# Attention: q and k from one projection of 128 stationary columns, and weight subtraction in four pieces

## What is computed

```python
def _L0_conv_ref(x, Wq, bq, Wk, bk, Wv, bv, alpha):      # B, C, H, W = 4, 256, 32, 32; MID = C // 8 = 32
    xf = x.reshape(b, c, n)
    q = jnp.einsum('mc,bcn->bmn', Wq, xf) + bq[None, :, None]
    k = jnp.einsum('mc,bcn->bmn', Wk, xf) + bk[None, :, None]
    v = jnp.einsum('oc,bcn->bon', Wv, xf) + bv[None, :, None]
    energy = jnp.einsum('bmi,bmj->bij', q, k)
    wmat = jax.nn.softmax(energy, axis=-1)
    y = jnp.einsum('bcj,bij->bci', v, wmat)
    return alpha[0] * y + x
...
t = t + _L1_attn_ref(_ln_t(t), L1_attn_proxy)
t = t + _L1_ffn_ref(_ln_t(t), gate_w, w1, b1, w2, b2)    # 8 experts, 2 for each token
```

## Time and profile before

| | us |
|---|---|
| median of 3 runs | 785.04 (781.91 to 786.17) |
| profiled execution, its own time | 785.2 |
| its span, first to last instruction | 783.5 |
| first instruction of stage B (SyncE's load, line 796) | at 221.23 |
| busy: PE, DVE, ACT, POOL | 714.9, 441.9, 331.9, 407.3 |

### The profile page before, as it was taken

How to read it: one execution, slowest core, us unless ns; L and a number is a source line. 1 busy time by engine, 2 the same in 40 slices (tenths; PEclk the granted TensorE clock), 3 DMA queues, 4 the chain that set the end, 5 groups by cost and what they waited for, 6 DMA issues and landing times.

```text
span 783.5 us, 18460 instructions
## 1 busy us (share of the span) xinstructions
PE 714.9 (91%) x5438; PEld 679.2 (87%) x5439; DVE 441.9 (56%) x1049; ACT 331.9 (42%) x640; POOL 407.3 (52%) x480
## 2 busy tenths in 40 slices
PE   5899999999939887489999999999999999999993
PEld 4899898998917665379999999999999999999993
DVE  3675666757636999625454554455454454454541
ACT  2674755747516677333323323323233233233230
POOL 1474565787662443263456556555565465555233
PEclk9999999999969999679999999999999999999997
DMA  7759578496460333222656535665476275373122
GB/s 244 244 175 399 216 264 341 165 352 248 162 256 28 111 109 110 83 77 76 209 157 195 183 82 177 182 197 155 149 236 173 48 227 177 53 225 79 20 29 30
DMA packets 45872, 130.14 MB, mean 166 GB/s; under 512 B 5184, under 2 KB 35520, under 8 KB 41216
## 3 DMA queue, kind: packets, MB, share of 16 engines
q1 hardware_dynamic: 30560, 104.86, 36.1%
q0 software_dynamic: 13904, 19.45, 14.3%
q10 hardware_dynamic: 1360, 5.24, 1.7%
HBM read 186.80 MB, written 47.59 MB: 299 GB/s over the span
## 4 chain that ended last, share of the span: by engine, by line
PE 54%; issue 1%; DMA 1%; POOL 1%; DVE 0%; POOLq 0%; ACT 0%; DVEq 0%
PE ps_h L73 9%; PE ps_h L74 9%; PE ps_h L75 9%; PE ps_y L73 8%; PE ps_y L74 8%; PE ps_y L75 8%; PE ps_x L1599 2%; DMA out_tok<-y,to_row 0%; POOL out_tok L1474 0%; DMA x_rows<-normed,from_row 0%; POOLq L1397 0%; DVE yb L1554 0%; DVE xtl L1534 0%; DVE y L1561 0%; ACT xth L1499 0%
## 5 line engine op out<-in xcount | busy, mean ns | idle before, releaser
L1508 ACT ACTIVATE g<-ps_h,bias 128x256 f32<-128x256 f32 x288 | 120.7, 471 | 279.5 <-PE ps_h L75 279.4
L1474 POOL DMA_INDIRECT out_tok<-y,to_row x72 | 126.9, 1762 | 140.2 <-DVE y L1561 119.7
L73 PE MATMUL ps_h<-xth,wbuf 128*128 128x256 f32 x576 | 164.6, 286 | 3.3 <-issue 1.8
L73 PE MATMUL ps_y<-wbuf,gl 128*128 x576 | 164.5, 286 | 0.0
L74 PE MATMUL ps_h<-xtl,wbuf 128*128 128x256 f32 x576 | 164.4, 285 | 0.0
L75 PE MATMUL ps_h<-xth,wbuf 128*128 128x256 f32 x576 | 163.1, 283 | 0.0
L75 PE MATMUL ps_y<-wbuf,gh 128*128 x576 | 161.6, 281 | 0.0
L74 PE MATMUL ps_y<-wbuf,gh 128*128 x576 | 161.6, 281 | 0.0
L73 PEld LDWEIGHTS ps_h<-xth,wbuf 128*128 128x128 f32 x576 | 109.6, 190 | 3.7 <-issue 2.1
L75 PEld LDWEIGHTS ps_h<-xth,wbuf 128*128 128x128 f32 x576 | 110.9, 193 | 0.0
L74 PEld LDWEIGHTS ps_h<-xtl,wbuf 128*128 128x128 f32 x576 | 109.8, 191 | 0.0
(11 more groups left out here) (241 smaller groups left out, 1297.0 us busy)
## 6 DMA issues: line engine op xcount, KB each, us to landing
wbuf<-wsplit SPq DMA_DIRECT2D x71, 2048.0 KB, 8.1
wsplit<-wbuf SPq DMA_DIRECT2D x14, 2048.0 KB, 12.0
wraw<-in_w SPq DMA_DIRECT2D x16, 1024.0 KB, 7.6
raw<-in_x_ch ACTq DMA_DIRECT2D x5, 1024.0 KB, 9.0
normed<-x SPq DMA_DIRECT2D x8, 528.0 KB, 3.0
tok<-in_x_tok SPq DMA_DIRECT2D x1, 4096.0 KB, 16.7
out_tok<-tok SPq DMA_DIRECT2D x8, 512.0 KB, 3.8
x_rows<-normed,from_row POOLq DMA_INDIRECT x72, 3.4
```

What stands on the lines that cost most here:

```text
L73: eng.matmul(out, ll, rh, start=first, stop=False)
L1474: pool.indirect_dma_start(out=out, out_offset=bass.IndirectOffsetOnAxis(ap=to_row[:, par, s:s + 1], axis=0), in_=y[:, par, s, :], in_offse ...
L1508: last = act.activation(g[:, f, :], ps_h[:, q, f % 2, :], ACT.Gelu_apprx_tanh, bias=bias1[:, bass.ds(e, 1), f:f + 1].rearrange("p a f -> p ...
```

## The change

One matrix of 128 stationary columns, Wq twice and Wk twice, replaces the two of 96. One projection of 12 matmuls gives all of q and k in `ps_sc`: rows 0 to 63 hold q twice, rows 64 to 127 hold k twice. It stands before the weighted sum of tile 6; the second projection, before tile 7, is gone, and `ps_pt[0]` isn't used for it. ScalarE makes the high parts with two activations of 64 partitions, both before the last weight part of the image. VectorE makes the low part of q in rows 32 to 63 and copies its high part to rows 64 to 95; it makes the low part of k in rows 64 to 95 and copies the high part, which stands in rows 96 to 127, to rows 0 to 31 and 32 to 63. That is three copies of 32x1024 for each image that were not there. Apart from that, GpSimd's subtraction of the weights is cut into four instructions of 128x512, the last of which signals.

```diff
@@ stage_a
-        wqh, wql = sb("wqh", [P, 2, KT, 3 * MID], F32R), sb("wql", [P, 2, KT, 3 * MID], F32R)
+        wqh, wql = sb("wqh", [P, KT, P], F32R), sb("wql", [P, KT, P], F32R)
-        qk3 = sb("qk3", [3 * MID, 2, N], F32R)
+        qk3 = sb("qk3", [P, 2, N], F32R)
@@ sync
-            for kind in range(2):
-                sp.dma_start(wq_raw[:, kind], wqk3[kind].rearrange("(k p) m -> p k m", p=P)).then_inc(wqk_in, 16)
+            sp.dma_start(wq_raw, wqk4.rearrange("(k p) m -> p k m", p=P)).then_inc(wqk_in, 16)
@@ gpsimd
-                        pool.tensor_tensor(wbuf[:, par, at + n:at + 2 * n], wraw[:, part],
-                                           wbuf[:, par, at:at + n].bitcast(F32), ALU.subtract).then_inc(w_lo, 1)
+                        m = n // PIECES
+                        for i in range(PIECES):
+                            last = pool.tensor_tensor(wbuf[:, par, at + n + i * m:at + n + (i + 1) * m],
+                                                      wraw[:, part, i * m:(i + 1) * m],
+                                                      wbuf[:, par, at + i * m:at + (i + 1) * m].bitcast(F32), ALU.subtract)
+                        last.then_inc(w_lo, 1)
@@ scalar
-            def high_qk(b, kind):
-                act.wait_ge(qk_mm, done(b * 2 + kind))
+            def high_qk(b):
+
+                act.wait_ge(qk_mm, done(b))
                 act.wait_ge(scored, done(b * IT - 1))
-                act.activation(qk3[:, kind], (ps_sc, ps_pt[0])[kind][0:3 * MID, :], ACT.Identity,
-                               bias=bqk[:, kind:kind + 1]).then_inc(qk_hi, 1)
+                for kind in range(2):
+                    at = slice(kind * 2 * MID, (kind + 1) * 2 * MID)
+                    act.activation(qk3[at, kind], ps_sc[at, :], ACT.Identity, bias=bqk[at, 0:1]).then_inc(qk_hi, 1)
@@
                     if it == 7 and more:
-                        high_qk(b + 1, 0)
+                        high_qk(b + 1)
@@
-                if more:
-                    high_qk(b + 1, 1)
@@ vector
-                at = slice(MID, 2 * MID) if kind == 0 else slice(2 * MID, 3 * MID)
+                low = slice((kind + 1) * MID, (kind + 2) * MID)
+                src, copies = ((0, (2,)), (3, (0, 1)))[kind]
                 dve.wait_ge(qk_hi, done(b * 2 + kind))
-                dve.scalar_tensor_tensor(out=qk3[at, kind], in0=(ps_sc, ps_pt[0])[kind][at, :], scalar=bqk[at, kind:kind + 1],
-                                         in1=qk3[at, kind].bitcast(F32), op0=ALU.add, op1=ALU.subtract).then_inc(qk_ok, 1)
+                dve.scalar_tensor_tensor(out=qk3[low, kind], in0=ps_sc[low, :], scalar=bqk[low, 0:1],
+                                         in1=qk3[low, kind].bitcast(F32), op0=ALU.add, op1=ALU.subtract)
+                for row in copies:
+                    last = dve.tensor_copy(qk3[row * MID:(row + 1) * MID, kind], qk3[src * MID:(src + 1) * MID, kind])
+                last.then_inc(qk_ok, 1)
@@ tensor
                 for n in range(N // HALF):
                     cols = slice(n * HALF, (n + 1) * HALF)
                     for k in range(KT):
-                        last = mm3(pe, dst[0:3 * MID, cols], (wqh[:, kind, k], wql[:, kind, k]),
-                                   (xh[:, k, cols], xl[:, k, cols]), k == 0, k == KT - 1)
+                        last = mm3(pe, ps_sc[:, cols], (wqh[:, k], wql[:, k]), (xh[:, k, cols], xl[:, k, cols]),
+                                   k == 0, k == KT - 1)
@@
-                        last = pe.matmul(ps_sc[:, cols], qk3[:, 0, it * P:(it + 1) * P], qk3[:, 1, cols],
+                        last = pe.matmul(ps_sc[:, cols], qk3[0:3 * MID, 0, it * P:(it + 1) * P], qk3[0:3 * MID, 1, cols],
@@
-                    if more and it >= IT - 2:
-                        project_qk(b + 1, it - (IT - 2))
+                    if more and it == IT - 2:
+                        project_qk(b + 1)
                     weigh(it)
@@ kernel
-        "wqk3": np.stack([np.tile(wq.T, (1, 3)), np.tile(wk.T, (1, 3))]),
+        "wqk4": np.concatenate([wq.T, wq.T, wk.T, wk.T], axis=1),
```

More of the change, by code:

```diff
@@ L42 @@
 EARLY = 2
+PIECES = 4
 FT = F // P
@@ L182, in chunk_tiles, with build @@
     return chunk_of(tok.t[:, :, :], c)[:, :, 0:C]
-def build(nc, x_ch, x_tok, wqk3, bqk3, wv_t, wv, bv, bv_t, alpha, proxy_t, gate_t, w1, b1_t, w2, b2, out):
+def build(nc, x_ch, x_tok, wqk4, bqk4, wv_t, wv, bv, bv_t, alpha, proxy_t, gate_t, w1, b1_t, w2, b2, out):
     wsplit = nc.dram_tensor("wsplit", [E, P, WROW], F32, kind="Internal").ap()
@@ L202, in build @@
         stage_a(nc, sem, tok, wbuf, ident, fixed, xraw, wsplit, normed, proxy_t, gate_t,
-                x_ch, x_tok, wqk3, bqk3, wv_t, wv, bv, bv_t, alpha, w1, w2)
+                x_ch, x_tok, wqk4, bqk4, wv_t, wv, bv, bv_t, alpha, w1, w2)
         tabs = keep("tabs", [P, 7, PAIRS], I32)
@@ L211, in stage_a @@
 def stage_a(nc, sem, tok, wbuf, ident, fixed, xraw, wsplit, normed, proxy_t, gate_t,
-            x_ch, x_tok, wqk3, bqk3, wv_t, wv, bv, bv_t, alpha, w1, w2):
+            x_ch, x_tok, wqk4, bqk4, wv_t, wv, bv, bv_t, alpha, w1, w2):
     with ExitStack() as ctx:
@@ L218, in stage_a @@
         xh, xl = sb("xh", [P, KT, N], F32R), sb("xl", [P, KT, N], F32R)
-        wqh, wql = sb("wqh", [P, 2, KT, 3 * MID], F32R), sb("wql", [P, 2, KT, 3 * MID], F32R)
-        bqk = sb("bqk", [3 * MID, 2])
+        wqh, wql = sb("wqh", [P, KT, P], F32R), sb("wql", [P, KT, P], F32R)
+        bqk = sb("bqk", [P, 1])
         wvh, wvl = sb("wvh", [P, KT, VW], F32R), sb("wvl", [P, KT, VW], F32R)
@@ L239, in early @@
             return wraw[:, 1, at:at + n].rearrange(spec, **sizes)
[L241 to L244, removed]
+        wq_raw = early(0, [KT, P], "p (k m) -> p k m", k=KT)
+        wv_raw = early(KT * P, [KT, VW], "p (k m) -> p k m", k=KT)
+        wv_nat = early(KT * P + KT * VW, [KT, C], "p (k m) -> p k m", k=KT)
+        zero_row = early(KT * P + KT * VW + KT * C, [PAD // P, XW], "p (k m) -> p k m", k=PAD // P)
         ps_sc = ctx.enter_context(nc.psum_tensor("ps_sc", [P, N], F32))
@@ L279, in _ @@
             sp.dma_start(bv_col, bv_t).then_inc(ext_in, 16)
-            for kind in range(2):
-                sp.dma_start(wq_raw[:, kind], wqk3[kind].rearrange("(k p) m -> p k m", p=P)).then_inc(wqk_in, 16)
-            sp.dma_start(bqk[:, :], bqk3).then_inc(consts, 16)
+            sp.dma_start(wq_raw, wqk4.rearrange("(k p) m -> p k m", p=P)).then_inc(wqk_in, 16)
+            sp.dma_start(bqk[:, :], bqk4).then_inc(consts, 16)
             sp.dma_start(wv_raw[:, :, 0:C], wv_t.rearrange("(k p) m -> p k m", p=P)).then_inc(consts, 16)
@@ L470, in _ @@
             act.wait_ge(consts, 64)
-            high_qk(0, 0)
-            high_qk(0, 1)
+            high_qk(0)
             images(act, image)
@@ L484, in _ @@
             last.then_inc(bv_spread, 1)
-            dve.wait_ge(wqk_in, 32)
-            dve.tensor_copy(wqh[:, :, :, :], wq_raw).then_inc(wsm_hi, 1)
+            dve.wait_ge(wqk_in, 16)
+            dve.tensor_copy(wqh[:, :, :], wq_raw).then_inc(wsm_hi, 1)
             dve.wait_ge(wsm_hi, 1)
-            dve.tensor_tensor(wql[:, :, :, :], wq_raw, wqh[:, :, :, :].bitcast(F32), ALU.subtract).then_inc(wsm_ok, 1)
+            dve.tensor_tensor(wql[:, :, :], wq_raw, wqh[:, :, :].bitcast(F32), ALU.subtract).then_inc(wsm_ok, 1)
             for k in range(KT):
@@ L613, in _, with project_qk @@
             pe.wait_ge(ident_ok, 1)
[L615 to L622, removed]
+            def project_qk(b):
+                pe.wait_ge(x_split, b + 2)
+                pe.wait_ge(exped, done(b * IT - 1))
                 for n in range(N // HALF):
@@ L686, in image @@
                         turn(it + 1)
-                    if more and it >= IT - 2:
-                        project_qk(b + 1, it - (IT - 2))
+                    if more and it == IT - 2:
+                        project_qk(b + 1)
                     weigh(it)
-            project_qk(0, 0)
-            project_qk(0, 1)
+            project_qk(0)
             pe.wait_ge(wsm_ok, 2)
@@ L1647, in _ @@
             all_pairs(pe, run)
-INPUTS = ["x_ch", "x_tok", "wqk3", "bqk3", "wv_t", "wv", "bv", "bv_t", "alpha", "proxy_t", "gate_t", "w1", "b1_t", "w2", "b2"]
+INPUTS = ["x_ch", "x_tok", "wqk4", "bqk4", "wv_t", "wv", "bv", "bv_t", "alpha", "proxy_t", "gate_t", "w1", "b1_t", "w2", "b2"]
 def kernel(x, L0_conv_Wq, L0_conv_bq, L0_conv_Wk, L0_conv_bk, L0_conv_Wv, L0_conv_bv, L0_conv_alpha,
@@ L1663 @@
         "x_tok": flat.transpose(0, 2, 1).reshape(TOK, C),
-        "wqk3": np.stack([np.tile(wq.T, (1, 3)), np.tile(wk.T, (1, 3))]),
-        "bqk3": np.stack([np.tile(np.asarray(L0_conv_bq), 3), np.tile(np.asarray(L0_conv_bk), 3)], axis=1),
+        "wqk4": np.concatenate([wq.T, wq.T, wk.T, wk.T], axis=1),
+        "bqk4": np.concatenate([np.asarray(b) for b in (L0_conv_bq, L0_conv_bq, L0_conv_bk, L0_conv_bk)])[:, None],
         "wv_t": wv.T,
```

## The result

The changed kernel takes 791.13 us (median of 5 runs, 789.77 to 792.23), the kernel before 785.27 us (5 runs, 781.91 to 786.17) beside it: ratio 1.0093, 95% interval 1.0069 to 1.0118. It is slower by 5.9 us. The prediction was 788.5, in a range of 783 to 794. It called a result above 789.0 slower and gave that 0.40, against 0.51 for the same: 791.13 is on the slower side. The profiled execution took 790.25 us, with a span of 788.5.

What follows compares the result with a forecast made beforehand. TensorE, busy 43.56 of 45 us, was taken to bound the attention stage. Start -0.3, passages between images +0.95, +0.95, +0.5 and end +1.4 sum to +3.5 on 785.04: 788.5 us, range 783 to 794.

Steps and rivals of the forecast that it cites:

- the clock: TensorE's new waits: granted clock drops to 0.50, one drop costing about 2 us, 790.5 to 792; chance 0.10.
- The projection: TensorE, each image: one of two 12-matmul projections goes, 128 columns cost nothing extra; 2.8 us saved, 11 us in all.
- The order at a passage: From one image to the next: engine times from t0, the image's last transposes; TensorE ends v's first part at +12.2, then waits.
- Do the copies wait for GpSimd?: Between images: VectorE copies wait for GpSimd's running piece, at most 1.29 us each; taken as +0.95, +0.95, +0.5.
- Rival 1: Between images: copies run beside GpSimd without collision; -1.6 us in all, 783.6; chance 0.20.
- rival 3: Between images: GpSimd isn't interrupted, copies wait through all four pieces; about +11.5 us, 796.5; chance 0.12.
- Rival 2: Between images: q and k ready before TensorE asks, near -2.1 us each; -5.2 in all, 780; chance 0.08.
- The second maximum 5.1 us after q and k are ready: Next image's start: VectorE's second row maximum comes 5.1 us after q and k are ready, against t0 +19.05 before.
- The start: Start of the attention stage: smaller weight split, then VectorE's row; q and k ready at 22.9 against 23.18, -0.3 us.
- The end: End of the attention stage: three GpSimd subtractions in series, 0.45 us longer each, +1.4 us before the next stage.

Runs made afterwards that it cites:

- filled_wait: Changed kernel plus 45 unread TensorE matmuls, 9 before each image's first score and 9 after the first projection; 786.43 us, ratio 1.0025 to the kernel before.
- scalar_moves: Changed kernel, VectorE's copies replaced by two more ScalarE activations from PSUM, last weight part ahead of them, subtraction whole; 778.24 us, ratio 0.9928 to the kernel before.
- no_copies: Changed kernel without the three VectorE copies, scores multiplying one 32-row group by itself, real scores left out; 784.3 us, ratio 1.0006 to the kernel before.

## Why the prediction came out as it did

The direction, the places and the new waits were right, and the time lies in the range, 2.6 us above the forecast. But the larger part of the loss, the clock, is no term of the sum: it was a rival. The nearness is partly luck: the stage lost 7.6 us where 3.5 were foreseen, and the rest of the profiled execution was 2.6 us shorter for no reason in the code. With the clock kept up the forecast's own terms come to +2.4 (the column of filled_wait in its table), less than its 3.5.

- **The projection.** Right: 12 matmuls of 128 stationary columns, from 60.59 until the next one starts at 63.43, 2.84 us against 2.86 with 96. The time that this frees went into waits, at the first passage 0.53 and 1.99 us. TensorE was to be 11 us less busy; in the stage it is 196.38 us busy in place of 199.60, 3.2 less, since its matmuls last longer at the lower clock; in scalar_moves, where the clock falls once, it is 9.6 less.
- **The order at a passage.** Right nearly line by line. From t0: ScalarE's weight part +4.14 (said: +4.1), its wait for the load 4.91 (4.51 + 0.45 = 4.96), tile 7's split +6.14 (+6.1), the q split +7.82 (+7.8), the k split +10.43 (+10.3), TensorE's wait for the split 0.53 (0.6), its end with v +12.47 (+12.2).
- **Do the copies wait for GpSimd?** They do, each side for a whole instruction of the other. Rival 1 had 783.6 and falls; rival 3 falls as well, as no copy took over 1.66 us beside pieces. Rival 2's condition, q and k in time, is met in scalar_moves: its passages are 2.2, 2.5 and 2.9 us shorter than before's, for the 2.1 that the rival gave. The size was near: ready at +14.41, +14.36 and +14.58, where +14.9, +14.9 and +14.45 were taken. The q copy won its tie with GpSimd each time, and the pair of k copies waited once and not twice: 1.3 us for both. By the rule that the prediction quoted from the Trainium skill (SBUF — State Buffer, section Who interferes with whom), a copy in the mode with both ports is shut out for a whole instruction: the trace agrees, with 5.02 us for a copy of 0.69, and with none for copies from PSUM; no row names the mode that a copy ran in.
- **The second maximum 5.1 us after q and k are ready.** Right at full clock: 5.04 and 4.97 at the second and third passage of filled_wait, 5.61 at the first, where VectorE waits 0.90 for GpSimd's part of v. In the changed kernel it is 6.50, 6.43 and 6.38.
- **The clock.** This is the step that failed, as the rival with 0.10. The prediction named the new waits, the drop and its price of "about 2 us", but gave one drop a small chance. There were four, at 0.9 to 1.6 us each, 5.3 in all: more than all other terms together. It had taken for its measure, a pause without end, and expected up to 3 us of wait at a passage; here the clock fell behind 2.0 us at each of three passages, each with a wait of 0.5 to 0.7 us some 5 us ahead of it. Its sign was off too: it looked for a score at half speed behind the first wait, and that pair took 0.73 us, as before; the fall came about 1 us later. The trace of before does not show how short a pause may be: in its attention stage from 24 us on TensorE's waits are 1.2 us at most, and the granted clock there is 1.00:

```profile
PE ps_o L73 <- DVE ptl L526: 4.7, 4, 1.2
...
24.00:200.00 176.00, 170.42 (x1225) 159.94 (x1223) 117.19 (x194) 112.25 (x144) 115.20 (x73) 1.00 0.73 269
```

  So in that trace waits of 1.2 did no harm, and a pause without end did; the new waits lay between. The rival should have had a much larger chance, since the forecast itself contained a wait of 1 to 4 us at all four places.
- **The start.** The order was right (first score at 22.77 against 23.18, -0.41, said -0.3); the clock turned it into +1.14.
- **The end.** +0.95 for +1.4. The pieces cost about 0.4 for each of the three subtractions as said (by the prediction's own figures, four times 1.28 less three overlaps of 0.04, they come to 5.0 and not 5.1; measured are 5.04), but the load landed 0.3 us sooner. The pieces alone gave +1.87 there.

What stays open: how short a pause brings the clock down, and what else decides. The 0.5 us wait ahead is not needed: in no_copies the clock fell at the start behind one pause of 2.21 us, with TensorE at work without a break for 8 us before it (its matmuls of 512 columns 0.43 us apart in the first half of them and 0.23 after). In the same run it fell behind a wait of 1.20 us once, and did not behind three waits of 1.20 to 1.28, so the length of the pause alone does not decide it. Pauses of other lengths were not tried on purpose.

## What to carry to other kernels

Work saved on the bounding engine is worth nothing if what it waits for becomes longer in the same stretch, and the pause then costs twice: once as a wait, and once at half clock with TensorE at work again. Look for who can make the copy on its way: here the engine that reads the source from PSUM anyway wrote it to both places, off the path, and the single projection became 0.7% faster in place of 0.9% slower. Where a pause can't be removed, matmuls that nobody reads bring back the second part of its price (the ratio here went from 1.0093 to 1.0025).

## What the hardware showed that I had not expected

- A pause of TensorE of 2.0 us, at all three passages, is followed by a granted clock of 0.50. Most of the slow time falls on work behind the pause: at the first passage the wait ended at 74.25 and the stretch 75 to 78 is at 0.50, with TensorE busy 3.00 of 3.00 us. When it falls varies: the first pair of scores behind the pause took 0.73 us at the first passage, 0.99 at the second and 1.22 at the third.
- Once, in no_copies, the clock fell behind a wait of only 1.20 us.
- Scores with 32 rows instead of 96 made a tile longer, 4.79 us in place of 4.43.
- The exclusion of VectorE's SBUF-to-SBUF copies and GpSimd works both ways, and at instruction boundaries: with 1.29 us pieces a pair of copies took 2.68 us and the four pieces 6.14 in place of 5.04; with one piece of 4.61 us a copy of 0.69 took 5.02.
- A copy of 32 partitions takes 0.69 us, as one of 128, and a copy of the same rows out of PSUM 1.28.
